# A graph network on one core: the node phase's fp32 products with the turned node features, each written as three fp16 products

## What is computed

```python
edge_attr = swish(edge_attr_raw @ enc_W + enc_b)
for _ in range(4):
    e_in = concatenate([edge_attr, x[src], x[dst]])             # 50000 x 384
    edge_attr = edge_attr + layernorm(swish(e_in @ eW1 + eb1) @ eW2 + eb2, eg, ebeta)
    agg = segment_sum(edge_attr, dst)                           # 3125 x 128
    n_in = concatenate([x, agg])                                # 3125 x 256
    x = x + layernorm(swish(n_in @ nW1 + nb1) @ nW2 + nb2, ng, nbeta)
out = layernorm(x0 + x)
```

## Time and profile before

| | us |
|---|---|
| three runs: median (lowest to highest) | 2530.68 (2520.82 to 2542.60) |
| the profiled execution, its own time | 2528.01 |
| its span | 2526.3 |
| busy: PE, DVE, ACT, POOL | 2357.6, 2216.7, 1912.4, 1623.0 |
| edge phases of steps 0 to 3, about | 71 to 659, 743 to 1257, 1342 to 1855, 1941 to 2455 |
| node phases of steps 0 to 3, about | 659 to 743, 1257 to 1342, 1855 to 1941, 2455 to 2526 |

### The profile page before, as it was taken

The page is one execution under the profiler, slowest core; times in us unless marked ns, Lnnn a source line. Parts: engine busy times, 40 slices in busy tenths (PEclk is TensorE's granted clock), DMA queues, the critical chain, the costliest instruction groups (busy, mean ns, idle before and its releaser), DMA issues.

```text
span 2526.3 us, 82599 instructions
## 1 busy us (share of the span) xinstructions
PE 2357.6 (93%) x27988; PEld 1848.9 (73%) x27988; DVE 2216.7 (88%) x6127; ACT 1912.4 (76%) x5248; POOL 1623.0 (64%) x1588
## 2 busy tenths in 40 slices
PE   5799999999979999999988999999997999999995
PEld 2577777777747787888765787888874788878874
DVE  7699999999747999999965999999984899999997
ACT  3577777777548888888846888888864888888884
POOL 2677777777117777777505777777712777777750
PEclk9899999999989999999999999999998999999998
DMA  5666666666347888888626888888834666676640
GB/s 167 180 203 204 202 201 203 207 204 205 101 150 217 254 253 253 256 255 262 214 98 192 254 256 254 258 257 254 254 126 159 201 205 203 205 207 203 207 144 27
DMA packets 382921, 515.14 MB, mean 204 GB/s; under 512 B 58581, under 2 KB 256356, under 8 KB 382490
## 3 DMA queue, kind: packets, MB, share of 16 engines
q1 hardware_dynamic: 303572, 302.15, 37.3%
q0 software_dynamic: 75264, 205.62, 28.9%
q10 hardware_dynamic: 3654, 1.99, 0.3%
HBM read 390.48 MB, written 119.05 MB: 202 GB/s over the span
## 4 chain that ended last, share of the span: by engine, by line
PE 39%; POOL 26%; DVE 15%; issue 10%; DMA 7%; ACT 2%; DVEq 0%; ACTq 0%; SPq 0%; POOLq 0%
POOL arena L1646 26%; PE psum L1687 8%; PE psum L1714 7%; PE psum L1675 7%; DMA arena<-node_tables,idx_all 7%; DVE arena L1942 3%; PE psum L1745 3%; PE psum L2142 3%; PE psum L1667 3%; PE psum L1699 2%; PE psum L2181 2%; DVE arena L1962 2%; PE psum L2155 2%; DVE arena L1901 2%; PE psum L1709 1%
## 5 line engine op out<-in xcount | busy, mean ns | idle before, releaser
L1646 POOL DMA_INDIRECT arena<-node_tables,idx_all x1568 | 1609.8, 1027 | 812.0 <-issue 424.9
L1811 ACT ACTIVATE arena<-psum 128x1024 f16<-128x1024 f32 x392 | 401.1, 1023 | 399.3 <-PE psum L1687 399.3
L1901 DVE SCALAR_TENSOR_TENSOR arena<-psum,arena 128x1024 f16<-128x1024 f32 x392 | 478.0, 1219 | 156.8 <-PE psum L1714 89.0
L1714 PE MATMUL psum<-w_hi,arena 128*128 128x128 f16 x6272 | 589.4, 219 | 3.9 <-DVE arena L1901 3.9
L1714 PE MATMUL psum<-w_lo,arena 128*128 128x128 f16 x3136 | 545.6, 219 | 0.0
L1714 PEld LDWEIGHTS psum<-w_hi,arena 128*128 128x128 f16 x6272 | 498.2, 98 | 17.2 <-DVE arena L1901 5.5
L1687 PE MATMUL psum<-arena,w_hi 128*128 128x512 f16 x1568 | 470.4, 382 | 1.4 <-ACT arena L1848 1.3
L1675 PE MATMUL psum<-ident,arena 128*128 128x128 f16 x6272 | 418.6, 220 | 39.5 <-DMA arena<-node_tables,idx_all 38.2
L1675 PEld LDWEIGHTS psum<-ident,arena 128*128 128x128 f16 x6272 | 378.8, 98 | 69.9 <-DMA arena<-node_tables,idx_all 62.2
L1824 ACT ACTIVATE arena<-psum 128x128 f32<-128x128 f32 x1568 | 412.6, 290 | 5.5 <-PE psum L1714 5.5
L1812 ACT ACTIVATE psum<-psum 128x1024 f32<-128x1024 f32 x392 | 399.5, 1019 | 0.0
(11 more groups left out here) (177 smaller groups left out, 3130.1 us busy)
## 6 DMA issues: line engine op xcount, KB each, us to landing
state<-arena SPq DMA_DIRECT2D x294, 256.0 KB
arena<-state SPq DMA_DIRECT2D x294, 256.0 KB
arena<-node_tables SPq DMA_DIRECT2D x784, 64.0 KB
arena<-matrices SPq DMA_DIRECT2D x294, 128.0 KB
node_tables<-arena SPq DMA_DIRECT2D x100, 256.0 KB, 2.2
arena<-node_tables,idx_all POOLq DMA_INDIRECT x1568
arena<-rel_rows SPq DMA_DIRECT2D x98, 128.0 KB
matrices<-arena SPq DMA_DIRECT2D x98, 128.0 KB
```

The source lines that it names most:

```text
L1646: pool.indirect_dma_start(out=rows[n % R][:, t, :], out_offset=None, in_=p_table, in_offset=bass.IndirectOffsetOnAxis(ap=idx_all[:, n % G1 ...
L1714: x = pe.matmul(ps_v(k2)[:, t * P:(t + 1) * P], h[k2][:, half, t * P:(t + 1) * P], w[:, half, :], start=False, stop=half == 1 and h is hl, ...
L1811: act.activation(hh[k2], ps_h(k2), ACT.Silu).then_inc(S("hh"), 1)
L1901: dve.scalar_tensor_tensor(hl[k2], ps_h(k2), 1.0, hh[k2], ALU.mult, ALU.subtract).then_inc(S("hl"), 1)
```

## The change

The turned nodes are kept as two fp16 halves in the place of the fp32 `xT_all`: `xT_hi` (ACT's copy, now with fp16 output) and `xT_lo` (the fp32 PSUM value less `xT_hi`, a new DVE operation). `w_pq` and the node half of `nw1` get fp16 high and low halves too (`w_pq16`, `nw1_16`), made once at the start by DVE. Each fp32 product with the turned nodes becomes three fp16 products: high by high, low by high, high by low. The product with `agg` stays fp32, and so does the second layer. PE waits for the new DVE operation (`xlo`, `tab_xlo`) where it waited for ACT's copy. In `tables` the turn of the chunk's fifth tile moves behind the first projection; ACT's copy of it moves behind the first high half. Two semaphores of the start are merged into `groupT`.

```diff
+        xT_hi = xT_all[:, 0:NPAD // 2].bitcast(F16)
+        xT_lo = xT_all[:, NPAD // 2:NPAD].bitcast(F16)
+        def project_nodes(pe, to, cols):
+            for x, w in ((xT_hi, 0), (xT_lo, 0), (xT_hi, 1)):
+                pe.matmul(to, x[:, cols], w_pq16[:, w, :], start=x is xT_hi and w == 0, stop=False, skip_group_check=True)
...
@@ in group_dve, ahead of pair_p_bias @@
+            all_pq = w_pq[:, :, :].rearrange("p k h -> p (k h)")
+            done2(dve.tensor_copy(w_pq16[:, 0, :], all_pq))
+            done2(dve.tensor_tensor(w_pq16[:, 1, :], all_pq, w_pq16[:, 0, :], ALU.subtract))
...
@@ in node_layer @@
+                done(dve.tensor_copy(nw1_16[:, 0, :], nw1[:, 0, :]))
+                done(dve.tensor_tensor(nw1_16[:, 1, :], nw1[:, 0, :], nw1_16[:, 0, :], ALU.subtract))
...
@@ begin_pe, project @@
-                    pe.wait_ge(Z("tab_xT"), t // TPG + 1)
+                    pe.wait_ge(Z("tab_xlo"), t // TPG + 1)
-                    pe.matmul(psum[:, t % R, :], xT_all[:, t * P:(t + 1) * P], w_pq[:, :, :].rearrange("p k h -> p (k h)"),
-                              start=True, stop=False, skip_group_check=True)
+                    project_nodes(pe, psum[:, t % R, :], slice(t * P, (t + 1) * P))
...
@@ begin_dve @@
+                def nodes_low(q):
...
+                    dve.wait_ge(Z("tab_xT"), q + 1)
+                    dve.tensor_tensor(xT_lo[:, cols], psum[:, 4 + q % 3, 0:(last - first) * P], xT_hi[:, cols],
+                                      ALU.subtract).then_inc(Z("tab_xlo"), 1)
                 for k in range(R):
                     dve.memset(at14[k][0:KA, :], 1.0).then_inc(Z("one"), 1)
+                nodes_low(0)
+                nodes_low(1)
                 matrices_of(0)
...
@@ its loop over tiles, behind the low half of tile t @@
+                    if t % TPG == 0:
+                        nodes_low(t // TPG + 2)
...
@@ Fast.dve @@
+                def low_table(c, t):
+                    if t == 1:
+                        turned_low(c, 1)
+                    table_low(c, t)
+                turned_low(0, 0)
                 update(2, nothing)
                 for t in range(CH):
                     low_table(0, t)
+                turned_low(1, 0)
                 update(3, nothing)
                 for t in range(CH):
                     low_table(1, t)
+                turned_low(2, 0)
                 update(4, lambda t: low_table(2, t))
                 for c in (3, 4):
+                    turned_low(c, 0)
                     for t in range(CH):
                         low_table(c, t)
...
@@ Node, hidden @@
-                        for k, rhs in enumerate((xT_all, agg)):
-                            x = pe.matmul(ps_n(c, j), nw1[:, k, m * P:(m + 1) * P], rhs[:, cols], start=k == 0, stop=k == 1)
-                        x.then_inc(S("hid"), 1)
+                        for x_part, w in ((xT_hi, 0), (xT_lo, 0), (xT_hi, 1)):
+                            pe.matmul(ps_n(c, j), nw1_16[:, w, m * P:(m + 1) * P], x_part[:, cols],
+                                      start=x_part is xT_hi and w == 0, stop=False, skip_group_check=True)
+                        pe.matmul(ps_n(c, j), nw1[:, 1, m * P:(m + 1) * P], agg[:, cols], start=False, stop=True,
+                                  skip_group_check=True).then_inc(S("hid"), 1)
...
@@ Node, tables on PE @@
+                    if c:
+                        pe.wait_ge(S("xlo"), 2 * b)
+                    for t in range(CH - 1):
+                        turn(t)
+                    pe.wait_ge(S("xlo"), 2 * b + 1)
                     for t in range(CH):
+                        if t == CH - 1:
+                            pe.wait_ge(S("xlo"), 2 * b + 2)
...
+                        project_nodes(pe, ps_p(t), slice(c * CW + t * P, c * CW + (t + 1) * P))
...
+                        if t == 0:
+                            turn(CH - 1)
...
@@ Node, tables on ACT @@
+                    turned(0)
                     for t in range(CH):
+                        if t == 1:
+                            turned(1)
                         act.wait_ge(S("pq"), CH * b + t + 1)
...
@@ Node, new on DVE @@
+                def turned_low(c, part):
...
+                    dve.wait_ge(S("xT"), 2 * b + part + 1)
+                    cols, tiles = turned_part(c, part)
+                    dve.tensor_tensor(xT_lo[:, cols], psum[:, 3, 0:tiles * P], xT_hi[:, cols], ALU.subtract).then_inc(S("xlo"), 1)
```

More of the change, by code:

```diff
@@ L119, in build_program @@
         w_pq = sb("w_pq", [P, 2, H], F32)
+        w_pq16 = sb("w_pq16", [P, 2, 2 * H], F16)
+        nw1_16 = sb("nw1_16", [P, 2, H], F16)
         nb1_col = sb("nb1_col", [P, 2], F32)
@@ L589, in weight_parts @@
             return first_layer, second_layer, node_layer, biases
[L591 removed]
+        W_OPS = 2 + 6 + 6 + 12
         d_row = sb("d_row", [1, H], F32)
@@ L679, in setup_pe @@
             pe.wait_ge(SU("width"), 1)
-            pe.transpose(psum[0:1, 0, 0:P], red[:, 3:4], ident32[:, :]).then_inc(SU("widthT"), 1)
+            pe.transpose(psum[0:1, 0, 0:P], red[:, 3:4], ident32[:, :]).then_inc(SU("groupT"), 1)
             pe.wait_ge(SU("flag"), 1)
@@ L702, in group_pe @@
             pe.wait_ge(SU("w"), NW)
-            pe.matmul(psum[0:1, 1, 0:H], beta_col[:, :], tmpw[:, 0:H], start=True, stop=True).then_inc(SU("betaw"), 1)
+            pe.matmul(psum[0:1, 1, 0:H], beta_col[:, :], tmpw[:, 0:H], start=True, stop=True).then_inc(SU("groupT"), 1)
         class Groups:
@@ L900, in nodes_turned @@
                     act.wait_ge(S("tab_turn"), t + 1)
-                    act.copy(xT_all[:, t * P:(t + 1) * P], psum[:, 6, 0:P]).then_inc(S("tab_xT"), 1)
+                    act.copy(xT_hi[:, t * P:(t + 1) * P], psum[:, 6, 0:P]).then_inc(S("tab_xT"), 1)
                 def tables_high(t):
@@ L965, in low_attributes, with nodes_low @@
                                       at16[g % 2][0:TPG * RAW + 1, :], ALU.subtract).then_inc(S("atlo"), 1)
+                def nodes_low(t):
+                    if t not in self.tiles:
+                        return
+                    dve.wait_ge(S("tab_xT"), t + 1)
+                    cols = slice(t * P, (t + 1) * P)
+                    dve.tensor_tensor(xT_lo[:, cols], psum[:, 6, 0:P], xT_hi[:, cols], ALU.subtract).then_inc(S("tab_xlo"), 1)
                 def tables_low(t):
@@ L983, in dve @@
                     matrices_of(g)
+                    if g % R == 0:
+                        nodes_low(g // R)
                     if g % R == 3:
@@ L1508, in turned @@
                     act.wait_ge(Z("tab_turn"), q + 1)
-                    act.copy(xT_all[:, first * P:last * P], psum[:, 4 + q % 3, 0:(last - first) * P]).then_inc(Z("tab_xT"), 1)
+                    act.copy(xT_hi[:, first * P:last * P], psum[:, 4 + q % 3, 0:(last - first) * P]).then_inc(Z("tab_xT"), 1)
                 silu, high = self.encode_acts(act)
@@ L1554, in begin_dve @@
                 matrices_of, low = self.first_matrices(dve)
+                def nodes_low(q):
+                    first, last = q * TPG, min((q + 1) * TPG, NT)
+                    if first >= NT:
+                        return
+                    dve.wait_ge(Z("tab_xT"), q + 1)
+                    cols = slice(first * P, last * P)
+                    dve.tensor_tensor(xT_lo[:, cols], psum[:, 4 + q % 3, 0:(last - first) * P], xT_hi[:, cols],
+                                      ALU.subtract).then_inc(Z("tab_xlo"), 1)
                 for k in range(R):
                     dve.memset(at14[k][0:KA, :], 1.0).then_inc(Z("one"), 1)
+                nodes_low(0)
+                nodes_low(1)
                 matrices_of(0)
@@ L2020, in slot @@
                         gains(n - 1)
-                update, low_table, last_norm, shift, add_root = node.dve_parts(dve, s)
+                update, table_low, last_norm, shift, add_root, turned_low = node.dve_parts(dve, s)
+                def low_table(c, t):
+                    if t == 1:
+                        turned_low(c, 1)
+                    table_low(c, t)
                 for g in range(G1 + 4):
@@ L2076, in ps_p, with turned_part @@
             return psum[:, (2, 6, 7)[t % 3], :]
+        def turned_part(c, part):
+            first, tiles = c * CW + part * (CH - 1) * P, (CH - 1, 1)[part]
+            return slice(first, first + tiles * P), tiles
         class Node:
@@ L2165, in tables, with turn @@
                         pe.wait_ge(S("xn"), a + 1)
-                    for t in range(CH):
-                        if t == CH - 1:
-                            pe.wait_ge(S("xT"), 2 * b + 1)
-                        elif t == 0 and c:
-                            pe.wait_ge(S("xT"), 2 * b)
+                    def turn(t):
                         x = pe.transpose(psum[:, 3, (t % 4) * P:(t % 4 + 1) * P], x_all[:, c * CH + t, :], ident32[:, :])
@@ L2220, in tables, with turned @@
                     _, b = self.counts(s, c)
```

(32 more changed lines are left out.)

24 lines of the change are left out of this document (9 added, 15 removed).

## The result

| | kernel before | kernel after |
|---|---|---|
| median of 20 runs each (lowest to highest) | 2533.15 (2520.82 to 2542.60) | 2544.09 (2538.88 to 2551.88) |
| the profiled execution, its own time | 2528.01 | 2541.21 |
| its span | 2526.3 | 2539.5 |

The ratio after/before is 1.0047 [1.0038, 1.0056]: some 12 us (10 to 14) slower, which is within 1%. The forecast was +10.5 us and 2541, the range 2522 to 2552.

The account below looks back on a forecast made before the run. PE bounds the first layer; in the tables the loop through ACT and DVE does. Start 0.5, three steps of 3.8, last step -1.4: +10.5 us, 2538.5 on the profiled execution, 2541 against the median, range 2522 to 2552.

Parts of the forecast that it names:

- Rival 6: Everywhere: a fp16 product is paced like half a fp32 one, 0.4 us more per projection; about +50 us, chance 0.01.
- rival 3: Whole kernel: everything that PE saves arrives, 2531 - 31 = 2500 us; chance 0.03.
- first layer: Steps 0 to 2: shorter node products bring the first turns 1.7 us early.
- chunks 1, 2 and 4: Table stages of steps 0 to 2: chunk 1 +0.65 (+0.15 with the first layer's saving), chunk 2 +0.1, chunk 4 0 us.
- chunk 3: Tables, steps 0 to 2: conversion queued behind `update(4)` makes the stage 2.3 us longer; 1.2 GHz afterwards adds 2.3 us.
- The walk through chunk 0: Tables, steps 0 to 2: conversion delays `update(2)` and the low halves that the fourth and fifth projections await; +0.65 us.
- Rival 4: Chunks 0 and 1: clock also falls behind waits of some 1.9 us before the first projection; +6.3 us, 2547; chance 0.11.
- The start: Before the first step: new conversions mostly hide in DVE's waits, PE's first projection comes 2.8 us later; +0.5, between 0 and +4.
- The last step: Step 3: cheaper first-layer products save 1.1 us plus half of chunk 4 and a little; -1.4 us.
- Rival 1: Chunk 3, steps 0 to 2: the clock holds behind its wait; +3.6 us, 2534; chance 0.18.
- Rival 2: Tables: conversions find cover, each chunk gains some 0.2 us and loses nothing; about -9 us, 2522; chance 0.12.
- Rival 5: Tables: the clock, once down in chunk 0, stays down through each step's tables; 34 us on top of +3.6, 2568; chance 0.05.

Follow-up runs that it names:

- e2: Kernel after without the new DVE conversions; the middle product reads the high half again and PE waits for ACT's copy: 0.9934 of before, 2509.21 us.
- e3: Kernel after with one DVE operation moved: chunk 3's conversion stands ahead of the scalings and addition of `update(4)`; ratio to before 1.0011.
- e6: Kernel after with each next chunk's turns, copies and conversions ahead of need and low halves woven into the updates: 0.9896 of before, 2496.98 us.
- e7: Same order as e6, but fp32 turned nodes, projections and first layer, with no conversions in the tables: 0.9945 of before, 2510.44 us.
- e4: Kernel after with 17 unused matmuls put into PE's wait ahead of chunk 3's first projection, to hold the clock: ratio to before 1.0023.
- e5: e3 with two low halves each of chunks 0 and 1 moved ahead of the scalings of `update(2)` and `update(3)`: ratio to before 0.9948.
- a0: The kernel after, unchanged, run again beside the others on one chip: ratio to before 1.0048, 2535.04 us.

## Why the prediction was right, and where it was not

**Bound and mechanism: right.** PE's saving in the tables was taken by the loop through DVE. e2 shows it from one side (without the conversions 29 us faster), e3 for chunk 3 alone (one conversion moved, 9 us), and e6 with e7 from the other: with conversions that come ahead of need the same products win 12 us over fp32.

**Prices of the products: right.** 0.41 and 0.65 us were forecast, 0.41 and 0.65 came (736.35 to 737.00). Rival 6 is out, and so is rival 3 (2500).

**Stages of a step.** For step 1 the table above has five of six within 0.2 us of the forecast: first layer -1.55 for -1.7, chunk 0 +0.60 for +0.65, chunks 1, 2 and 4 as said. All that is off is chunk 3: +3.4 for +4.6. The wait was 3.7 us for 4.3, and the step that failed in size is the clock's: "Three projections then take 1.5 us for 0.75, 2.3 us in all". Two projections and a turn were at 1.2 GHz, 727.69 to 730.87, 3.2 us for 1.6; e4 measures the difference at 1.43 us. The lateness was 1.94 (e4) for 2.3.

The walk through chunk 0 gave the right sum. Its times also give the wait ahead of the fourth projection: the first projection at about 695.3, three at a pace of 0.76 and the moved turn, the fourth at 699.96, so some 2.1 us; it measured 2.01. Rival 4 carries this wait as 1.2 us, and with 2.1 the 2.25 us that it adds to three projections would have been hidden nearly whole.

**Rival 4 came in part.** It put the loss in chunks 0 and 1 at 1.05 us each, in all six, behind the wait before the first projection. The clock fell behind the second wait, the 2.01 us before the fourth, and not each time: in 2 of 6 stages in each of the two profiles of the kernel after, 4 of 6 in e3, 3 of 6 in e4, where both waits are the same. A fall costs 1.5 to 1.7 us (stages of 12.9 to 13.0 for 11.36, 16.7 to 16.8 for 15.15), since it slows the second layer as well. The forecast kept the clock up there, on the ground that a wait of 1.07 us had not lowered it; it never priced the longer wait at the fourth projection. That this wait and not the 1.78 us before the first projection matters is borne out by e5, which has only the latter, and by e2 (1.06 and 1.67 us): no fall in six stages each.

So the +10.5 was right in part by luck, because two errors cancel: chunk 3 cost 3.4 us less over three steps (3.5, 3.4 and 3.5 for 4.6 each), and chunks 0 and 1 cost 2 x 1.6 = 3.2 us more in the profiles. In the runs it may have been more. The mean granted clock of the 20 runs of after is 0.9803, that of the profiled one 0.982; at half the clock, 0.0017 of 2540 us is twice that share, 8.6 us of low clock, some two or three falls more. That would fill the 2 to 4 us between node phases and ratio; it is argued from the mean, which also holds low stretches in which PE stands, and no timeline of those runs shows it. The gap stays open.

**The clock gate, by the page.** Chunk 3 fell in all six stages of the two profiles of after, behind 3.7 us. In the Trainium skill, page "TensorE: Matmul & The Clock Gate", section "HAM oscillation — how this bites in real kernels", each wait between short bursts brings the next burst back to the low clock; the waits of its kernel are some 3 to 5 us. For chunk 3, whose wait is of that length, the trace agrees. The 2.01 us in chunks 0 and 1 are shorter than the waits of that section, and behind them the clock fell in 11 of 24 stages (after, a0, e3, e4), so the forecast could not rest on the section there either way. Whether transposes ahead of a wait count as standing, no run here separates.

**The start.** +0.5 was taken, between 0 and +4. PE's first projection came 1.7 us later (32.55 for 30.81) and not 2.8. From the first scaled row of the matrices on DVE to the first gather it is 35.5 us in both kernels; the operations ahead of it hid in waits, as forecast, and the conversions in the loop cost nothing either. DVE at the start, after:

```profile
27.14 0.41 DVE L548 COPY beta_w<-psum 1x256 f32<-1x256 f32 x1 [1.31 <-PE psum L716]
...
31.79 1.21 DVE L1582 TENSOR_TENSOR xT_all<-psum,xT_all 128x512 f16<-128x512 f32 x2
...
35.22 0.48 DVE L1558 TENSOR_SCALAR arena<-arena,part_cmp 128x512 fp8e4<-128x512 f16 x1 [2.22 <-DMA arena<-rel_rows]
```

The 2.08 us wait shrank to 1.31, and the 3.33 us wait to 2.22, with the two conversions (1.21) where it was the earlier trace rows. First gathers came at 71.57, 71.72 and 72.41 before, at 70.72 and 69.42 after: no cost shows.

**The last step.** -1.4 was taken; it is -1.8 to -2.4 (67.28 and 67.63 against 69.47 to 69.67). Most of the first layer's 20 x 0.13 arrives there; the norms did not hide it.

**Rival 1** (clock holds in chunk 3) is e4's case, and e4 came at +6 for +3.6, with falls in 3 of the 6 stages of chunks 0 and 1. **Rival 2** (conversions find cover) is nearest to e6 against e7, where cover makes the change worth -12 us; e3 covers one conversion of a step and comes at +3, and e5's -13 is in part the order's own gain. **Rival 5** did not come: the clock is back within 3.2 us in chunk 3, and chunk 4's projections are at full pace.

## What to carry to other kernels

A cheaper product helps only where its engine is the one that the next stage waits for; here the three fp16 products were worth the same 12 us in either order, once as a loss and once as a gain, and what decided was where the turn, ACT's copy and DVE's conversion stood: ahead of need, or last in the path of the next projection, in chunk 3 behind an update that this projection had no use for. So before giving an engine a new operation on the way to PE, lay out where it would be queued, and move the operation (or what makes its input) ahead of that. And price each new wait twice, once for its length and once for the clock behind it, also a wait in the middle of a burst.

## What the runs showed of the hardware

- Behind a wait of 2.01 us, which itself follows a burst of three projections and a wait of 1.8 us, the clock fell in 11 of 24 stages and stayed in 13, with the same instructions ahead of it, at the same distances to 0.02 us. By the granted clock the fall comes 0.4 to 1.4 us after PE has gone on: in 5 of the 11 within the first projection and its bias, in 6 in the second. Waits of 1.78 us alone (e5) gave none in six stages.
- Behind 3.73 us the clock was low in all six stages of the two profiles of after. In three it was low when the first projection began, as at 727.69, and there full pace is back after 3.2 us (730.87); in two it fell 0.3 us later, in one 1.0 us later (a0, step 0).
- The sum of the edge phases differs by 9 us between executions whose code there is the same (2139.18 in e3, 2148.37 after). A single profile can't show a node-phase effect of a few us in its span; the stages can.
